# The decoder layer's start: T2 produced in the layout that A reads, T1's weights in two transfers, and separate homes for the last tile's FFN rows

## The reference: what is computed

```
Q, V = x Wq^T + bq, x Wv^T + bv                       # 16 heads of 16
w = softmax(top 4 of (Q . latent_keys) / 4)            # over 64 latent keys a head
x = layernorm(x + (sum of w * latent + V) Wo^T + bo)

q_big = (x Wq^T) w_kc_q ;  q_r = q_big W_qr            # 16 heads
k_r = rope(ctx) W_kr ;  p = softmax(q_r . k_r)         # over 64 context rows
x = layernorm(x + ((p rope(ctx)) w_kc_kv^T) Wo^T)

h = silu(lin(x, w1, g1)) * lin(x, w2, g2)              # 256 -> 1024
x = layernorm(x + lin(h, w3, g3))                      # 1024 -> 256
# lin: RMS norm with gain, rows rounded to whole numbers of 127, ternary weights
```

## Time and profile before

| | before |
|---|---|
| median of 3 runs | 338.94 us (338.52 to 338.99) |
| the profiled execution | 339.06 us |
| its span in the trace | 337.3 us |
| PE busy | 315.6 us, 94% |
| PE weight loads busy | 228.5 us, 68% |
| DVE busy | 280.3 us, 83% |
| ACT busy | 283.0 us, 84% |
| POOL busy | 247.9 us, 73% |
| granted TensorE clock | full in all slices |
| DMA busy | above 60% in the first 40 us, then mostly below 20% |

### The profile page before, as it was taken

One profiled execution on the slowest core, in us unless ns is written; L12 is line 12 of the kernel. 1 busy time (PEld: TensorE's weight loads), 2 busy tenths in 40 slices (PEclk: granted clock), 3 DMA queues, 4 the chain that ended last, 5 costly groups with the idle time before them and its releaser, 6 DMA issues. The chain is left out here.

```text
span 337.3 us, 7205 instructions
## 1 busy us (share of the span) xinstructions
PE 315.6 (94%) x2392; PEld 228.5 (68%) x2392; DVE 280.3 (83%) x717; ACT 283.0 (84%) x535; POOL 247.9 (73%) x234
## 2 busy tenths in 40 slices
PE   8999988999899998999999999999998999989972
PEld 4786766687777865777778757776685777466441
DVE  1497568957879999999997899999997878988882
ACT  2686899994759889989897999999896899998873
POOL 3367536884878997898889797969794965668661
PEclk9999999999999999999999999999999999999999
DMA  6999800000000001120101140020220213111001
GB/s 222 400 421 415 315 15 2 0 4 2 0 2 1 17 16 31 33 47 4 33 16 33 32 34 17 17 63 0 49 47 33 33 33 78 31 32 35 14 20 47
DMA packets 24853, 22.29 MB, mean 66 GB/s; under 512 B 19824, under 2 KB 22256, under 8 KB 23920
## 3 DMA queue, kind: packets, MB, share of 16 engines
q1 hardware_dynamic: 24816, 21.84, 21.2%
HBM read 15.01 MB, written 2.10 MB: 51 GB/s over the span
## 5 line engine op out<-in xcount | busy, mean ns | idle before, releaser
L589 PE MATMUL small<-V_sb,PT_sb 128*128 128x256 f32 x256 | 58.3, 381 | 0.8 <-ACT PT_sb L872 0.8
L589 PEld LDWEIGHTS small<-V_sb,PT_sb 128*128 128x128 f32 x256 | 48.0, 190 | 9.4 <-issue 2.5
L554 PE MATMUL wide<-B_sb,x1T 128*128 128x512 f32 x192 | 49.6, 407 | 2.9 <-ACT PT_sb L872 1.5
L1379 POOL TENSOR_TENSOR Ls<-Ls,m 128x1024 f32<-128x1024 f32 x16 | 31.2, 1948 | 26.9 <-DVE mask L1122 26.9
L1108 DVE MAX8 m<-Ls 128x8 f32<-128x64 f32 x256 | 33.9, 210 | 13.8 <-ACT Ls L802 13.5
L554 PEld LDWEIGHTS wide<-B_sb,x1T 128*128 128x128 f32 x192 | 35.4, 188 | 13.2 <-ACT PT_sb L872 3.1
L1444 POOL TENSOR_TENSOR region_c<-region_c,region_q 128x1024 f32<-128x1024 f32 (+1 forms) x17 | 33.3, 1959 | 9.1 <-DVE region_c L1233 6.8
L1394 POOL TENSOR_TENSOR Ls<-Ls,mask 128x1024 f32<-128x1024 f32 x16 | 37.9, 2366 | 2.5 <-ACT Ls L815 1.8
L1386 POOL TENSOR_TENSOR mask<-mask,r 128x1024 f32<-128x1024 f32 x16 | 32.3, 2019 | 2.6 <-DVE r L1131 2.5
L613 PE MATMUL wide<-tern,region_k 128*128 128x512 bf16 x128 | 32.6, 379 | 0.6 <-ACT region_k L926 0.3
L1417 POOL TENSOR_TENSOR P<-P,r 128x1024 f32<-128x1024 f32 x16 | 30.5, 1904 | 1.1 <-DVE r L1177 1.1
(11 more groups left out here) (190 smaller groups left out, 836.7 us busy)
## 6 DMA issues: line engine op xcount, KB each, us to landing
region_q<-in_wqx SPq DMA_DIRECT2D x1, 2048.0 KB, 17.6
region_c<-in_woTx SPq DMA_DIRECT2D x1, 2048.0 KB, 10.7
out_x<-region_q SPq DMA_DIRECT2D x16, 128.0 KB, 1.9
first<-in_xT SPq DMA_DIRECT2D x7, 256.0 KB, 8.6
region_c<-in_wkcqT SPq DMA_DIRECT2D x1, 1536.0 KB, 11.8
region_r<-in_wqkr SPq DMA_DIRECT2D x1, 1024.0 KB, 7.5
region_r<-in_w1T SPq DMA_DIRECT2D x1, 1024.0 KB, 12.8
region_t<-in_w2T SPq DMA_DIRECT2D x1, 1024.0 KB, 14.8
```

The costliest lines, as they stand in the source:

```text
L554: mm = pe.matmul(ps_L2[:, r * 512:(r + 1) * 512], x1T[:, u, k, :], B_sb[:, s, w, k, r * 512:(r + 1) * 512], start=(u == w == k == 0), stop ...
L589: mm = pe.matmul(ps_O2[:, 0:D], PT2_sb[:, c, :], V_sb[:, c, :], start=(c == 0), stop=(c == PAIRS - 1))
L1379: pool.tensor_tensor(heads(Ls[n % 2][:]), heads(Ls[n % 2][:]), over_heads(m8[:, :, 0:1]), ALU.subtract).then_inc(g_d1, 1)
```

## The change

Three edits, and small moves in PE's list.

- **T2.** The operands of `T2_` are swapped: w_kc_q is stationary (128 columns), T1 is moving (64 columns). For u = 0 the contraction runs over 128 rows, for u = 1 over 64 rows in two halves e, and u changes after every two matmuls. There are 32 matmuls as before. The output is laid out as `A_` reads it. `T2T` and `keep_T2` are gone; `copy_T2` waits for `T2_` itself, and stays behind `copy_PT1(0)` in ACT's list. T2's bank is now wide[1], the bank of `L1(1)`, so `T2_` waits until ACT has copied `L1(1)` out. In PE's list `warm(2)` ahead of `T1_(0)` is gone and `warm(5)` stands ahead of `T2_`.
- **T1's weights** come in two transfers of 512 KB, each with the matching head pairs of both weights; `T1_` waits for the second one only at its fifth pair.
- **Homes for tile 15.** `th`, `hh`, `hg`, `hqT`, `xg`, `xqT` and the bank of `XQT` have copies of their own for tile 15, in memory that is dead by then. The waits for tile 14 on these buffers fall, and waits for the dead memory's last readers come. `gate_2(15, 0)` has a reciprocal of one column more. `HT(13)` now waits for `copy_XQ(15)` (a_qT 4), since `XQT(15)` uses its bank; `warm(4)` instead of `warm(2)` stands ahead of it. No call changes its place.

The core of the diff:

```diff
-            sp.dma_start(region_r[:], a["wqkr"]).then_inc(ld_T1, 16)
+            for i in range(2):
+                sp.dma_start(halves_r[:, i], a["wqkr"][:, i]).then_inc(ld_T1[i], 16)
...
             def T1_(u, *freed):
                 bank_of(*freed)
-                pe.wait_ge(ld_T1, 16)
                 for c in range(PAIRS):
+                    i, ci = divmod(c, PAIRS // 2)
+                    if u == 0 and ci == 0:
+                        pe.wait_ge(ld_T1[i], 16)
...
             def T2_(*freed):
-                for i in range(PAIRS // 2):
+                for c in range(PAIRS):
                     for u in range(2):
-                        for e, c in ((0, i), (1, i + PAIRS // 2), (1, i), (0, i + PAIRS // 2)):
+                        for e in range(2):
                             h, rows = e * PAIRS + c, slice(e * DC, (e + 1) * DC)
-                            mm = pe.matmul(ps_T2[rows, c * HK:(c + 1) * HK],
+                            mm = pe.matmul(ps_T2[:, h * DC:(h + 1) * DC],
+                                           wkcqT[1][rows, c, :] if u else wkcqT[0][:, h, :],
                                            T1[1][rows, c * DC:(c + 1) * DC] if u else T1[0][:, h * DC:(h + 1) * DC],
-                                           wkcqT[1][rows, c, :] if u else wkcqT[0][:, h, :],
                                            start=(u == 0), stop=(u == 1))
...
-            def T2T(*freed):
...
-            def keep_T2():
...
+            def home(n, own, last):
+                return last if n == TILES - 1 else own
...
-            warm(2, wide[0], p_warm, 2); T1_(0, p_warm, 3); T1_(1, a_L1, 1); Q(1, a_Q, 1)
-            L1(1, a_T1, 2, a_L1, 1); T2_(a_T1, 1); WF(); PT1(0, a_T2k, 1); T2T(a_L1, 2)
-            Q(2, a_Q, 2); L1(2, a_T2, 1, a_L1, 2); A_(0, a_PT1, 1); WT(0, v_WF, 1); WB(a_Q, 3)
+            warm(9, wide[0]); Q(0); warm(4, wide[0], p_warm, 1); L1(0); T1_(0, p_warm, 2)
+            T1_(1, a_L1, 1); Q(1, a_Q, 1); L1(1, a_T1, 2, a_L1, 1); warm(5, wide[0], a_T1, 1)
+            T2_(a_L1, 2); WF(); PT1(0, p_warm, 3); Q(2, a_Q, 2); L1(2, a_T2, 1, a_L1, 2)
...
-            warm(7, wide[0], p_warm, 5); XQT(15, a_qT, 3); warm(2, wide[0], p_warm, 6)
-            HT(13, None, a_hT, 1); Z_(0, 15, 0, p_warm, 7); O3(12, a_qT, 4); Z_(0, 15, 1)
+            warm(7, wide[0], p_warm, 5); XQT(15, a_hT, 1); warm(4, wide[0], p_warm, 6)
+            HT(13, None, a_qT, 4); Z_(0, 15, 0, p_warm, 7); O3(12, a_qT, 3); Z_(0, 15, 1)
...
             def gate_2(n, half=None):
-                since(dve, a_sqh, n)
-                since(dve, g_hg, n)
+                if n < TILES - 1:
+                    since(dve, a_sqh, n)
+                    since(dve, g_hg, n)
+                if half == 0:
+                    dve.reciprocal(h_and_eps_last[:, FF:], root_eps_h[:])
...
             def gain_h(n, half=None):
-                since(pool, d_hT, 16 * min(n, TURNED))
-                since(pool, p_HT, n - TURNED)
+                if n < TILES - 1:
+                    since(pool, d_hT, 16 * min(n, TURNED))
+                    since(pool, p_HT, n - TURNED)
```

More of the change, by code:

```diff
@@ L368, in T1_ @@
                                ps_T1[1][rows, e * 512 + c * DC:e * 512 + (c + 1) * DC])
-                        mm = pe.matmul(dst, wqrT[rows, c, 0:P] if u == 0 else wqrT[rows, c, P:DCQ],
-                                       wkrT[rows, c, :], start=True, stop=True)
+                        mm = pe.matmul(dst, wqrT[rows, i, ci, 0:P] if u == 0 else wqrT[rows, i, ci, P:DCQ],
+                                       wkrT[rows, i, ci, :], start=True, stop=True)
                 mm.then_inc(p_T1, 1)
@@ L612, in Z_ @@
                     for k in range(KD):
-                        mm = pe.matmul(inner(w, half)[:, r * 512:(r + 1) * 512], xqT[:, w * KD + k, :],
+                        mm = pe.matmul(inner(w, half)[:, r * 512:(r + 1) * 512], home(n, xqT, xqT_last)[:, w * KD + k, :],
                                        tern12[:, w, k, r * 512:(r + 1) * 512],
@@ L906, in whole_x2 @@
                 act.wait_ge(v_sq, n + 1)
+                rows = home(n, xg, xg_last)
                 for k in range(2):
-                    ins = act.activation(xg[:, k, :], xg[:, k, :], ACT.Copy, bias=ROUND,
+                    ins = act.activation(rows[:, k, :], rows[:, k, :], ACT.Copy, bias=ROUND,
                                          scale=sq[:, k:k + 1])
@@ L924, in copy_XQ @@
                 act.wait_ge(p_XQT, n + 1 - TURNED)
[L925 to L926 removed]
+                if n < TILES - 1:
+                    since(act, p_Z2, n)
+                else:
+                    act.wait_ge(p_O1, 12)
+                act.activation(home(n, xqT, xqT_last)[:],
+                               home(n, xqT16, xqT16_last).rearrange("p (k t) -> p k t", k=2 * KD), ACT.Copy,
                                bias=-HALF_BIAS).then_inc(a_qT, 1)
@@ L939, in tanh @@
                 act.wait_ge(v_tq, n + 1)
-                since(act, v_g2, n)
                 if n == 0:
                     act.wait_ge(p_C, 2)
-                act.activation(th[:, columns(half)], inner(0, half)[:, columns(half)], ACT.Tanh,
+                if n < TILES - 1:
+                    since(act, v_g2, n)
+                else:
+                    act.wait_ge(p_O1, 12)
+                    act.wait_ge(g_P1, TILES)
+                act.activation(home(n, th, th_last)[:, columns(half)], inner(0, half)[:, columns(half)], ACT.Tanh,
                                scale=tq[:, n % 3, 0:1]).then_inc(a_tanh, 1)
@@ L955, in whole_h @@
                 act.wait_ge(v_sqh, n + 1)
-                act.activation(hg[:, columns(half)], hg[:, columns(half)], ACT.Copy, bias=ROUND,
+                row = home(n, hg, hg_last)[:, columns(half)]
+                act.activation(row, row, ACT.Copy, bias=ROUND,
                                scale=ch[:, 2:3]).then_inc(a_qh, 1)
@@ L961, in copy_HT @@
                 act.wait_ge(p_HT, nth(n, half) - TURNED)
-                since(act, p_O3, n)
+                if n < TILES - 1:
+                    since(act, p_O3, n)
                 src = hT16 if half is None else hT16_last[half]
-                act.activation(hqT.rearrange("p c t -> p (c t)")[:, columns(half)], src[:, columns(half)],
+                act.activation(home(n, hqT, hqT_last).rearrange("p c t -> p (c t)")[:, columns(half)], src[:, columns(half)],
                                ACT.Copy, bias=-HALF_BIAS).then_inc(a_hT, 1)
@@ L1220, in gate_1 @@
                 dve.wait_ge(a_tanh, nth(n, half))
-                dve.scalar_tensor_tensor(th[:, cols], th[:, cols], 1.0, inner(0, half)[:, cols], ALU.add, ALU.mult
+                row = home(n, th, th_last)[:, cols]
+                dve.scalar_tensor_tensor(row, row, 1.0, inner(0, half)[:, cols], ALU.add, ALU.mult
                                          ).then_inc(v_g1, 1)
@@ L1239, in largest_h @@
                 dst = ch[:, 0:1] if half is None else peaks[:, half:half + 1]
-                dve.tensor_reduce(dst, hg[:, columns(half)], AX, ALU.max, apply_absolute_value=True
+                dve.tensor_reduce(dst, home(n, hg, hg_last)[:, columns(half)], AX, ALU.max, apply_absolute_value=True
                                   ).then_inc(v_amh, 1)
```

99 lines of the change are left out of this document (53 added, 46 removed).

## The result

The changed kernel takes **347.79 us** (median of 4 runs, 344.97 to 348.63), the kernel before 338.88 beside it (338.52 to 338.99): a ratio of 1.025 [1.0189, 1.0311], 8.9 us slower. The forecast was 342.1 with a range of 339.7 to 343.0. Its direction holds; its size and its range do not. The profiled execution took 347.18 us, 345.5 of them span.

What follows compares the result with a forecast made beforehand. The prediction took PE's queue in the start to bound the kernel. L1(2) +3.1 us (+0.64 + 3.0 - 0.87 + 0.39) and tail +0.1 on 339.06 gave 342.3, taken as 342.1 us, range 339.7 to 343.0.

Steps and rivals of the forecast that it cites:

- The forecast's L1(2): On PE behind T2_: L1(2) starts at 28.6 us instead of 25.49, 3.1 us later, and everything after it too.
- The forecast's own sum for this start: T2_'s start on PE: L1(1) at 14.08, then ACT's copy and semaphore, giving 16.05 us, 0.64 later than before.
- The prediction's signs of being wrong: In the timeline: T2_ under 6 us, or L2(0) starting less than 2.5 us later, would refute the forecast.
- T2_'s mechanism and its two prices: In T2_: 0.1115 us per 128-column load, 0.145 per change of form; 0.96 per c, 7.7 in all against 4.68.
- The price of a change of form: On PE, switching between full array and row halves costs about 0.145 us; T2_ has 16 changes instead of 8.
- rival 2: In T2_'s 48 steps: moving columns set the pace, T2_ takes 3.3 us, kernel faster at 337.8 us; chance 6%.
- The wait for copy_T2: Ahead of L1(2): waiting for ACT's copy_T2 eats 0.39 of T2T's saved 0.87 us; L1(2) 4.91 us after WF's start.
- keep_T2 brought nothing by leaving: On ACT: removing keep_T2 saves nothing, since nothing there waited for its time.
- rival 3: Behind L1(2): the delay doesn't reach the end, or the tail's freed buffers pay it back; 338.9 us, chance 8%.
- The tail: Tile 15: freed waits gain nothing, the reciprocal holds gate_2 by 0.08 us, HT(13)'s delay is covered; sum +0.1 us.
- The part ahead of T2_: Start on PE: without warm(2), T1_(0) starts at 9.15 instead of 9.82; T1_(1), Q(1), L1(1) follow 0.67 us earlier.
- Rival 4: In T2_: full-array loads aren't hidden behind matmuls; T2_ takes 10.2 us, L1(2) 5.7 later, 344.7 us; chance 5%.

Runs made afterwards that it cites:

- e10: The changed kernel with three matmuls of zeros inside T2_, after c = 1, 3 and 5: 343.19 us, ratio 1.0122.
- e4: The changed kernel with seven matmuls of zeros inside T2_, one after each c but the last: 343.49 us, ratio 1.0129.
- e3: The changed kernel with T2_'s loops turned, all 128-row matmuls first, then all 64-row ones (2 changes of form instead of 16): 341.91 us, ratio 1.007.
- e1: The kernel before with the T2 edit alone; warm(2), single load of T1's weights and shared buffers stay: 347.33 us, ratio 1.0232.
- e2: The changed kernel with the old T2 stage put back (T2_, keep_T2, T2T, A_), all other edits kept: 338.45 us, ratio 0.9976.
- e5: The kernel before with the last tile's own homes alone: 339.03 us, ratio 0.9996.
- e7: The changed kernel with T2_'s loops turned, T2 in wide[0], no warm(5), copy_T2 ahead of exp_4(1) on ACT: 338.84 us, ratio 0.999.
- e8: The changed kernel with seven more matmuls of zeros ahead of T2_ (warm(12) for warm(5)), none inside: 347.65 us, ratio 1.0251.
- e6: The kernel before with T1's weights in two transfers and without warm(2), nothing else: 338.38 us, ratio 0.9988.
- e9: The changed kernel with 128 moving columns instead of 64 in T2_ except its last c, same loads and changes of form: 344.1 us, ratio 1.0136.

## Why the prediction was right and wrong

**The step that failed is one that the sum doesn't have: the clock.** Each duration of the forecast came from rows at the full clock, and I carried them into T2_ and WF as if the clock were given. No term and no rival has it, and the prediction gives no reason for leaving it out. The forecast's L1(2) is 16.05 + 7.7 + 4.91 = 28.66; it came at 33.57, 4.91 us later. By terms:
- T2_ began at 16.41, not 16.05: +0.36. T1_(0) started at 9.54, not at 9.15; the group ahead of it all, Q(0), took 2.75 us in this execution and 2.36 in that of before, though both began at 5.05. (The forecast's own sum for this start, 14.08 + 0.79 + 1.09 + 0.07, is 16.03; the 16.05 is 0.02 too much.)
- T2_ took 10.34, not 7.7: +2.64, all of it in the part after the clock fell, since the first four c took 0.957 us each.
- WF took 3.58, not 1.83: +1.75. Nothing of it was edited. The prediction moved it and priced it at nothing.
- From PT1(0) to L1(2) 3.24, not 3.08: +0.16, the first part of it still at the lower level.

So 4.4 of the 4.9 us are the clock in two terms. Put into the sum, 342.3 + 4.9 is 347.2, and the profiled execution took 347.18. e10 and e4 show it from the other side: with the clock held, the pieces of T2_ cost what was forecast. The prediction's signs of being wrong missed it too: a T2_ under 6 us and an L2(0) less than 2.5 us later. Both look for too little delay, and none says how much would be too much.

**T2_'s mechanism and its two prices were right.** 0.96 us for each c against 0.957, at the full clock. The price of a change of form came out of e3 at 0.144 us against 0.145. By the starts of the loads in the changed kernel, at the full clock, the full group took 0.587 us (forecast 0.59) and the half group 0.369 (0.37). A 128-column load does set the pace over 64 moving columns here, against rival 2. The Trainium skill (TensorE: Matmul & The Clock Gate, LDWEIGHTS) has a load's time go with the stationary's columns and not with its rows; the traces agree in the spacing of the loads, with 0.1115 us for T1_(0)'s 64 rows and (0.587 - 0.145) / 4 = 0.11 for T2_'s 128, both 128 columns wide.

**The wait for copy_T2 was right.** ACT's timeline of the changed kernel, two rows:

```profile
31.58 1.02 ACT L826 ACTIVATE PT_sb<-wide 128x1024 f32<-128x1024 f32 x1 [9.93 <-PE wide L495]
32.50 1.02 ACT L733 ACTIVATE PT_sb<-wide 128x1024 f32<-128x1024 f32 x1
```

copy_PT1(0) begins 1.25 us after PT1(0), with a slower PT1(0), copy_T2 0.92 after that, and L1(2) starts on its end, after 0.30 us of waiting on PE. That keep_T2 brought nothing by leaving was forecast too; no run tests it alone.

**The delay reached the end in full,** as forecast, against rival 3. The span less L1(2)'s start is 311.8 us before and 311.9 after; in e1, e2, e3, e4, e5, e7, e8 and e10 it lies between 311.9 and 312.1. Only e6 and e9 have more, 313.3 and 313.4, and those are the two whose transposing transfer was late. So this start tells the whole kernel's time, but for such a transfer, and nothing behind it gave the delay back.

**The tail** was forecast at +0.1. The rows of PE, DVE and POOL that answer to the earlier trace rows:

```profile
329.28 1.06 PE L648 MATMUL small<-tern,region_k 128*128 128x257 bf16 x8 [0.40 <-ACT region_k L979]
...
331.86 0.15 DVE L1251 RECIPROCAL first<-root_eps_h 128x1 f32<-128x1 f32 x1
331.93 0.73 DVE L1252 SCALAR_TENSOR_TENSOR first<-wide,tq,mask 128x512 f32<-128x512 f32 x1
...
332.74 2.65 POOL L1468 TENSOR_TENSOR first<-first,region_q 128x512 f32<-128x512 f32 x2 [1.61 <-DVE first L1252]
333.28 0.75 DVE L1252 SCALAR_TENSOR_TENSOR first<-wide,tq,mask 128x512 f32<-128x512 f32 x1
```

O3(13) still had 0.40 us of waiting ahead of it, so the later HT(13) was covered. The reciprocal holds gate_2 by 0.07 us. gain_h(15) starts at once on its gate, as the change wants, and the second half still waits for its own gate, so the earlier start was worth nothing, as forecast. What the forecast doesn't have: the two halves take 2.65 us instead of 2.19, and most of that is no waiting, since each half now lasts 1.27 us instead of 1.09. It is so in all nine traced kernels with the new homes (1.27 to 1.28) and in none of the three without (before, e1, e6). From the end of gate_2(15, 1) to the end of the span they take 11.42 to 11.44 us instead of 11.35 to 11.37. The size of +0.1 thus fits, in part for a cause that wasn't in it; why POOL is slower on the new home isn't shown. e5 puts the whole of the homes within 0.2% of nothing.

**The part ahead of T2_** was right where it can be seen alone: e2 and e6 start T1_(0) without warm(2) and bring L1(2) 0.73 and 0.69 us forward, where the forecast had 0.67 for that part. e6 is the clean case, with L1(0) at 8.46 against 8.49 before; in e2 all of the start came 0.5 us earlier and most of that was lost again at T1_, so its 0.73 agrees in part by luck.

**Rival 4** (10.2 us for T2_, from loads that don't hide) named nearly the time that T2_ took, 10.34, and isn't its cause: the first four c of T2_ are free of it, and so is all of T2_ in e10. A total that fits says little; the two halves of the same loop told the causes apart.

**The cause of the fall.** That T2_ brings it is shown: it comes with T2_ alone (e1), goes with it (e2), and doesn't go with more work ahead (e8). All twelve runs of the changed kernel, e1 and e8 have a mean clock of 0.978 to 0.989, all ten of e2 0.995 or more. T2_ isn't the only place for it, though: e4's trace has a fall in T1_, and one run in twelve of e6, with the old T2_, has 0.988. What in T2_ brings it is shown as far as this: more moving columns under the same loads (e9) or a few wide matmuls among them (e10, and e4 with the reserve named there) hold the clock in the traces and go with a mean clock of 0.993 or more in all twelve runs of these three kernels. That little is streamed beside the loads is my reading of it. The Trainium skill (TensorE: Matmul & The Clock Gate, What's actually happening) says that a monitor sets the clock by how busy TensorE has been. By the profile's rows PE was busy for all of each slice in which the clock fell, so if the page holds here, "busy" there isn't what the profile's busy column counts. Why e3, with the same columns and loads in 5.65 us, keeps its clock in the trace and perhaps not in each run stays open.

## What to carry to other kernels

Before a duration is carried into an edited stage, ask what clock it was read at and whether the new stage will hold it. Here a long stretch of wide weight loads with a short moving side left TensorE busy by the profile and still went with a fall of its clock, and the unchanged work behind it paid too (1.75 of 8.08 us). When two operands can be swapped, compare both sides: with the wider one moving the same product took 4.68 us, with it stationary 7.66 at the full clock, or 5.65 with only two changes of form. Count the changes of form, and where such a stretch can't be avoided, try a few wide matmuls inside it, not ahead. Where a whole program is a chain behind one engine's early work, a single start time read early tells an edit's effect apart from a disturbance elsewhere: here L1(2) gives the end within 0.4 us in ten of twelve traces, and the other two show the late transfer.

## What the runs showed of the hardware that I had not expected

- **The clock fell while PE was never idle.** From about 20.4 to 30.6 us PE ran at 1.2 GHz with busy rows of 4.00 in 4.00 us. WF, eight f32 matmuls of 256 columns, took 1.83 us at the upper level and 3.58 at the lower.
- **It can happen in T1_ too.** In e4's profiled execution T1_, with 64 moving columns as well, took 4.55 us instead of 3.08, with a mean clock of 0.85 from 8 to 12 us and 0.72 from 12 to 16. There it had waited 0.79 us for its weights; in e5 a wait of 0.51 us left it at 3.08. What decides this isn't settled. The changed kernel has the same T1_ and takes 3.08 us for it in its trace.
- **The start differs between executions of the same work.** Q(0) took 2.36 us before, 2.75 after and 1.89 in e5, all ahead of anything that was edited. The traces' first record of the full clock comes in the same order, at 5.98, 6.79 and 4.67 us. This fits a Q(0) that begins at the lower clock and is sped up on its way, although the clock column shows 1.00 there. When Q(0) is early, T1_ waits for its weights instead (0.51 us in e5), so only part of the difference goes on: L1(2) of e5 starts 0.19 us earlier than before.
- **A transposing transfer was 1.7 us late in two of twelve profiled executions** (e6, e9), and each time the span was 1.4 us longer. This is as large as most effects looked for here, and is why the start times decided more than the medians did.
- **The same POOL instruction was slower on another buffer.** Each half of gain_h(15) took 1.27 us on its new home and 1.09 on the old one. What makes it so stays open.
